# Two-layer adaptive FFN with adapters: the low parts of the token blocks are formed by VectorE instead of GpSimd

## What is computed

```
x = x + ffn0(cond0(x))
    cond0: per item one of 8 weight matrices 512x512 (chosen by itok_B_3_7)
    ffn0:  x @ kernel + bias + per-group low-rank part + shared low-rank part
x = x + ffn1(cond1(x))
    cond1: gate = x @ Wg.T + 0.5*lora ; up = x @ Wu.T + 0.5*lora
           act = silu(gate) * up      ; down = act @ Wd.T + 0.5*lora
           (width 1376; per item one of 16 adapters of rank 16, itok_B_2_6)
    ffn1:  h @ W.T + b + a low-rank part whose rank (8, 16, 32, 64) a router picks per token
```

## Time and profile before

| what | value |
|---|---|
| median of 3 runs | 784.7 us (783.61 to 786.11) |
| the profiled execution, its own time | 782.29 us |
| span of the profiled execution | 780.5 us |
| TensorE busy | 754.0 us, 97% of the span |
| GpSimd busy | 394.7 us, 51% |
| ScalarE busy | 277.3 us, 36% |
| VectorE busy | 272.6 us, 35% |
| mean granted TensorE clock | 0.999 |

### The profile page before, as it was taken

The page is one execution under the profiler, slowest core; times in us unless marked ns, Lnnn a source line. Parts: engine busy times, 40 slices in busy tenths (PEclk is TensorE's granted clock), DMA queues, the critical chain, the costliest instruction groups (busy, mean ns, idle before and its releaser), DMA issues.

```text
span 780.5 us, 11119 instructions
## 1 busy us (share of the span) xinstructions
PE 754.0 (97%) x3902; PEld 625.1 (80%) x3902; DVE 272.6 (35%) x459; ACT 277.3 (36%) x431; POOL 394.7 (51%) x334
## 2 busy tenths in 40 slices
PE   3789999999999999999999999999999999999998
PEld 2567886888888878888888778888888788888885
DVE  4595554421111555211112663111115452111134
ACT  3441262443332424533332435333323334333222
POOL 2177548486674304776664035866642147766500
PEclk9999999999999999999999999999999999999999
DMA  6955455244432331434434041434332324433201
GB/s 261 413 188 190 149 189 217 54 129 122 121 106 85 119 135 40 121 121 121 121 83 165 11 164 60 137 105 121 121 110 78 134 63 128 119 98 120 75 1 55
DMA packets 30873, 96.59 MB, mean 124 GB/s; under 512 B 4832, under 2 KB 4960, under 8 KB 28800
## 3 DMA queue, kind: packets, MB, share of 16 engines
q1 hardware_dynamic: 20544, 61.12, 23.8%
q0 software_dynamic: 10304, 35.14, 14.0%
HBM read 86.28 MB, written 9.96 MB: 123 GB/s over the span
## 4 chain that ended last, share of the span: by engine, by line
PE 90%; DMA 3%; DVE 2%; POOL 2%; issue 1%; ACT 1%; SPq 0%; ACTq 0%; DVEq 0%
PE psD L994 11%; PE psD L995 10%; PE psD L996 10%; PE psG L994 7%; PE psG L996 7%; PE psG L995 7%; PE psU L994 7%; PE psU L996 7%; PE psU L995 7%; PE psD L1055 2%; PE psD L1056 2%; PE psD L1057 2%; DMA xs<-in_x,idx_g 2%; DMA gu_raw<-in_gu 1%; PE psT L996 1%; PE psT L995 1%
## 5 line engine op out<-in xcount | busy, mean ns | idle before, releaser
L440 POOL TENSOR_TENSOR gu_lo<-gu_raw,gu_hi 128x1024 fp32r<-128x1024 f32 x44 | 105.7, 2403 | 180.9 <-ACT gu_hi L566 180.6
L480 POOL DMA_INDIRECT ab<-in_ab,idx_row x88 | 85.9, 976 | 47.7 <-POOL idx_row L474 34.3
L906 DVE TENSOR_TENSOR act_f<-psU,silu 128x512 f32<-128x512 f32 x44 | 30.4, 691 | 222.6 <-PE psU L996 216.5
L680 ACT ACTIVATE silu<-psG 128x512 f32<-128x512 f32 x44 | 26.3, 597 | 181.3 <-PE psG L996 181.1
L440 POOL TENSOR_TENSOR dn_lo<-dn_raw,dn_hi 128x512 fp32r<-128x512 f32 x44 | 56.8, 1291 | 39.3 <-ACT dn_hi L566 39.3
L994 PE MATMUL psG<-x_hi,gu_hi 128*128 128x512 f32 x176 | 72.9, 414 | 0.0
L996 PE MATMUL psG<-x_hi,gu_lo 128*128 128x512 f32 x176 | 69.2, 393 | 0.0
L994 PE MATMUL psD<-act_hi,dn_hi 128*128 128x512 f32 x176 | 69.0, 392 | 0.0
L995 PE MATMUL psD<-act_lo,dn_hi 128*128 128x512 f32 x176 | 69.0, 392 | 0.0
L994 PE MATMUL psU<-x_hi,gu_hi 128*128 128x512 f32 x176 | 68.9, 391 | 0.0
L995 PE MATMUL psG<-x_lo,gu_hi 128*128 128x512 f32 x176 | 68.7, 390 | 0.0
(11 more groups left out here) (264 smaller groups left out, 1837.3 us busy)
## 6 DMA issues: line engine op xcount, KB each, us to landing
gu_raw<-in_gu SPq DMA_DIRECT2D x44, 512.0 KB, 3.5
dn_raw<-in_dn SPq DMA_DIRECT2D x44, 256.0 KB, 2.6
cond_w_raw<-in_cond_w SPq DMA_DIRECT2D x8, 1024.0 KB, 13.1
tok<-h_scratch SPq DMA_DIRECT2D x4, 1024.0 KB, 6.0
x_t<-in_x_t SPq DMA_DIRECT2D x4, 1024.0 KB, 5.4
out_t<-out_b SPq DMA_DIRECT2D x16, 256.0 KB, 3.5
ab<-in_ab,idx_row POOLq DMA_INDIRECT x88, 3.1
lora_a<-in_lora_a SPq DMA_DIRECT2D x1, 1024.0 KB, 5.7
```

Source lines behind the costliest of these rows:

```text
L440: pool.tensor_tensor(dst, x, hi, ALU.subtract).then_inc(s, 1)
L480: pool.indirect_dma_start(ab[:, par, g, :], None, a["ab"], bass.IndirectOffsetOnAxis(idx_row[:, par, g:g + 1], 0)).then_inc(S[f"ab_in{par} ...
L680: act.activation(silu[:], psG[:], ACT.Silu).then_inc(S["silu_s"], 1)
L906: dve.tensor_tensor(act_f[:], psU[:], silu[:], ALU.mult).then_inc(S["act_f_s"], 1)
```

## The change

In the four token blocks VectorE now forms `gu_lo`, `bu_lo`, `dn_lo` and `bd_lo`. GpSimd keeps the indirect DMAs, `ae_lo`, and `wf_lo` and `ra_lo` in its prologue. VectorE gets the wait for `wf_lo_s` ahead of its first block. On VectorE `low_gu(0, ...)` stands between the last `x1_lo` and `ranks(0)`, `bd_lo` behind `ranks(1)`, and in each step `low_gu` of the next chunk stands ahead of `ad_lo`, and `dn_lo` behind it. The steps that VectorE runs outside its loop change from 0 and 1 to 1 and 2, plus the rest that the loop of four leaves. A local name is changed as well (`last` to `copied`), since `last(fc)` is now called there.

```diff
@@ gpsimd
             def body(t, more):
-                def low_gu(par, n):
-                    pool.wait_ge(S["gu_hi_s"], n + 1)
-                    low(gu_lo[:, par, :], gu_raw[:], gu_hi[:, par, :], S["gu_lo_s"])
-                    pool.wait_ge(S["bu_hi_s"], n + 1)
-                    low(bu_lo[:, par], ab[:, par, :, P:STAB], bu_hi[:, par], S["bu_lo_s"])
-
-                low_gu(0, NF * t)
-                pool.wait_ge(S["bd_hi_s"], t + 1)
-                low(bd_lo[:], fix[:, :, 2 * D:FIX], bd_hi[:], S["bd_lo_s"])
-
                 def step(fc, j, par):
                     n = NF * t + fc
-                    if not last(fc):
-                        low_gu(1 - par, n + 1)
-                    pool.wait_ge(S["dn_hi_s"], n + 1)
-                    low(dn_lo[:, par, :], dn_raw[:], dn_hi[:, par, :], S["dn_lo_s"])
                     if not last(fc) and not last(fc, 1):
@@ vector
             for c in range(C):
                 low_h0(0, c)
+            dve.wait_ge(S["wf_lo_s"], 1)
 
             def body(t, more):
...
+                def low_gu(par, n):
+                    dve.wait_ge(S["gu_hi_s"], n + 1)
+                    low(gu_lo[:, par, :], gu_raw[:], gu_hi[:, par, :], S["gu_lo_s"])
+                    dve.wait_ge(S["bu_hi_s"], n + 1)
+                    low(bu_lo[:, par], ab[:, par, :, P:STAB], bu_hi[:, par], S["bu_lo_s"])
...
+                low_gu(0, NF * t)
                 ranks(0)
                 low_at(3)
                 dve.wait_ge(S["tg_lo_s"], 2 * t + 1)
                 ranks(1)
+                dve.wait_ge(S["bd_hi_s"], t + 1)
+                low(bd_lo[:], fix[:, :, 2 * D:FIX], bd_hi[:], S["bd_lo_s"])
 
                 def step(fc, j, par):
                     n = NF * t + fc
+                    if not last(fc):
+                        low_gu(1 - par, n + 1)
                     dve.wait_ge(S["ad_hi_s"], n + 1)
                     low(ad_lo[:, par, :], psX[:, 0:NGT * P], ad_hi[:, par, :], S["ad_lo_s"])
+                    dve.wait_ge(S["dn_hi_s"], n + 1)
+                    low(dn_lo[:, par, :], dn_raw[:], dn_hi[:, par, :], S["dn_lo_s"])
                     dve.wait_ge(S["silu_s"], n + 1)
...
-                chunks(dve, step, 0, 1)
+                chunks(dve, step, 1, 2)
```

More of the change, by code:

```diff
@@ L958, in body @@
                 for k, hi in enumerate(RANKS):
-                    last = dve.tensor_copy(mexp[:, :, lo:hi],
-                                           soft[:, 10, :, k:k + 1].broadcast_to([P, SUB, hi - lo]))
+                    copied = dve.tensor_copy(mexp[:, :, lo:hi],
+                                             soft[:, 10, :, k:k + 1].broadcast_to([P, SUB, hi - lo]))
                     lo = hi
-                    last.then_inc(S["mexp_s"], 1)
+                    copied.then_inc(S["mexp_s"], 1)
                 dve.wait_ge(S["mask_ps"], SUB * (t + 1))
```

## The result

| | median | runs | ratio to before (95%) |
|---|---|---|---|
| before | 785.07 us | 783.61 to 786.11, 4 runs | |
| after | 795.91 us | 794.61 to 797.28, 4 runs | 1.0138 [1.0121, 1.0155] |

The change costs 10.8 us. The forecast was 794.3 with 9.6 us of loss and a range of 789.5 to 798. The profiled execution after has a span of 792.7 us and its own time is 794.61; before it was 780.5 and 782.29.

A forecast was written before the change was run, and what follows sets the result against it. TensorE was taken to bound the kernel. Terms of 3.5 + 0.7 + 5.4 = 9.6 us of loss, added to the 784.7 us median, gave 794.3 us, with a range of 789.5 to 798.

The forecast's parts named there:

- The bound: Blocks 1 to 3: TensorE busy throughout, nothing to win; its 3.0 us of block 0 waits is about all the gain.
- Place 1: VectorE's new wait for wf_lo ahead of block 0: TensorE stalls 6.9 us, less 3.4 of old waits, +3.5 us once.
- The start of `wf_lo`: GpSimd prologue: wf_lo may start 0.5 us earlier, as the gather ahead no longer meets r_lo; end taken as 127.15.
- Place 2: gu_lo(0) and bu_lo(0) ahead of ranks(0) on VectorE: TensorE's ranks(1) weight load late, 0.2 a block, +0.7 us for four.
- Place 3: ad_lo(0) behind bd_lo, gu_lo(1) and bu_lo(1) on VectorE: TensorE's turn_down waits 1.36 us a block, +5.4 us for four.
- Steps 2 to 10: Later chunk steps of each block: gu_lo(n+1) is ready a step early, cost 0.
- the load of `gu_raw`: SP's next gu_raw load, sent after gu_lo(0), goes out later but is covered with 2.0 us to spare, cost 0.
- GpSimd's freed time: Some 230 us of work removed from GpSimd, which no TensorE step waits for in steady state; worth nothing in itself.
- the gathers: GpSimd's gathers: VectorE subtractions delay them at most 1.3 us a time, hidden because they are issued earlier.

The follow-up runs named there:

- e3: Changed kernel with VectorE's wf_lo wait directly ahead of gu_lo(0), ad_lo ahead of gu_lo and bu_lo in every step, and bd_lo behind the chunks; 783.18 us.
- e8: Kernel before with bd_lo alone moved from GpSimd to VectorE, behind the chunks, no new wait for wf_lo; 782.93 us.
- e4: Kernel before with VectorE's wait for wf_lo ahead of block 0 as the only edit; 791.33 us.
- e2: Changed kernel with ad_lo ahead of gu_lo and bu_lo in every VectorE step and bd_lo behind the chunks, wf_lo wait left in place; 791.19 us.
- e1: Changed kernel with VectorE's wait for wf_lo moved from ahead of the block body to directly ahead of gu_lo(0); 789.8 us.
- e5: Changed kernel with bd_lo alone moved on VectorE from behind ranks(1) to behind the chunks; 791.4 us.
- e6: Changed kernel with dn_lo ahead of ad_lo in every step, one more instruction ahead of ad_lo(0); 798.25 us.
- e7: Changed kernel with GpSimd forming wf_lo between the gathers of the first and second chunk instead of behind both; 793.29 us.

## Why the prediction was right

**The bound.** TensorE's 100% in blocks 1 to 3 said that nothing could be won there. e3 and e8 bear it out: the best order tried of the same change gains 0.26%, and e3's 1.8 and e8's 2.4 us stay under the 3.0 us that the prediction gave as about all there is.

**Place 1** was forecast at +3.5. By the parts it was 6.7 us of stall (forecast 6.9), less 3.4 of old waits absorbed (as forecast), plus 2.4 us of matmuls at half the clock (6.46 - 4.04), which the sum didn't have: 5.7. By the whole of block 0 it is 6.0 (7.1 longer, less 1.1 at `ad_lo`). e4 says 6.4 for the wait alone; its trace has one later fall of the clock, and the slow stretch in block 0 was longer there (6.9 us from the first column to the second, where the kernel after has 6.46). Against e3, which has the order right, the wait costs e2 more, 8.0 by the medians (791.19 - 783.18) and 7.4 by the blocks, since e3 is 1.3 us under the kernel before in that block (164.1 against 165.5): with `bd_lo` gone from GpSimd block 0 waits less, and the stall hides that. The term that failed is the price of the stall: "a stall of 6.9 us" was priced as 6.9, and here each stall of TensorE cost its length and a stretch of slow matmuls behind it. That the fall of the clock comes with the stall is shown by e4, which adds the stall and gets the fall, and by e1 and e3, which take the stall away and lose it.

**The start of `wf_lo`.** The gather ahead of it took 0.95 us instead of 1.46, and `wf_lo` began 0.97 us after that gather's start, as forecast from the earlier trace rows. Counted from the first transposes of block 0 `wf_lo` ended 0.5 us earlier than before (12.53 against 13.06). The rule of the Trainium skill (SBUF — State Buffer, "Who interferes with whom") that a `tensor_tensor` leaves descriptor generation alone, which the page gives as inferred, doesn't fit here. In the kernel after a gather that began inside VectorE's `bd_lo` took 1.44 us (from two timelines):

```profile
158.46 1.44 POOL L480 DMA_INDIRECT ab<-in_ab,idx_row  x1 [0.30 <-issue]
...
157.86 1.22 DVE L700 TENSOR_TENSOR bd_lo<-fix,bd_hi 128x1024 fp32r<-128x1024 f32 x1
```

It isn't one row any more. Of the 88 `ab` gathers of the kernel after, 30 began while a VectorE subtraction with both inputs in SBUF was running that had 0.15 us or more to go. All 30 are longer (1.01 to 1.51 us), each by the rest of that subtraction less about 0.1; the other 58 took 0.95 to 0.99. In the kernel before there are two such gathers: the one of the earlier trace rows, and one that began only 0.02 us into a subtraction and isn't longer. In e4, where the wait moves `r_lo` away from the gathers, none is longer. Gathers that had begun before the subtraction aren't longer either. So the prediction's reading of that row holds. Why the page's inference fails isn't shown: a gather also reads its indices (`idx_row`) from SBUF, which may be what is held up. The page's other rule, that a VectorE instruction with two SBUF inputs and a GpSimd instruction that reads SBUF exclude each other, is what e8 shows (2.11 to 0.69 us).

**Place 2** was forecast at 0.7 in all and costs under 0.2. The last `at_lo` ended 5.08 us behind the last `x_lo`'s start (317.79 + 0.68 - 313.39), as computed (5.11). TensorE's `ranks(1)` began 5.21 us behind it, just as in the earlier trace rows and the profile before; the weight load came late by 0.15, and the matmul didn't, so the early start of the weight load was slack that I had counted as need.

**Place 3** was forecast at 1.36 a block and is 1.1, 4.4 in all where 5.4 was said. Mechanism and order are as told (`bd_lo`, `gu_lo(1)`, `bu_lo(1)`, then `ad_lo(0)`); the spacing behind a 1024-element subtraction is 1.14 us, not 1.20, which for the two of them is about half of the 0.27 a block that the forecast was too high; the rest lies between the end of `ad_lo` and TensorE's restart. e2, e5 and e6 show the mechanism.

**Costed at nothing, rightly.** Steps 2 to 10 (e3's block of 164.5 us), the load of `gu_raw`, which took part of its 2.0 us of slack (in block 0 `gu_hi(1)` and `bu_hi(1)` ended at 155.3, 1.3 us ahead of `tg_hi(1)`), GpSimd's freed time, the gathers.

**Sum.** 3.5 + 0.7 + 5.4 = 9.6 against 10.8. Two terms were 1.0 and 0.5 too large, one was 2.4 too small. That the total came within 1.2 us is in part luck: with places 2 and 3 at what they turned out to cost, the same working gives about 8.1, and the stretch at half clock is the 2.4 that it lacks.

## What to carry to other kernels

When work moves between engines that are not the bound, the sum of busy times says nothing. Take each wait of the bounding engine, measure how early it is met today, and count what newly stands in that queue ahead of the instruction that meets it: here 103 us of work cost nothing, and one instruction a block in the wrong place (`bd_lo`, e5) 4.4 us. A wait belongs right ahead of the instruction that needs it, since everything written behind it on that engine waits with it: moving this one down by a few lines brought 6 us (e1). And a stall of TensorE of several us is dearer than its length, by what its clock takes to come back: 2.4 to 3.1 us on stalls of 3.6 to 6.7 us here.

## What the runs showed of the hardware

- A pause of TensorE of 3.6 us (e7) already brought the granted clock from 1.00 to 0.50 before work resumed, and the matmuls then ran at half speed for about 5 us (0.63 us each instead of 0.39), much as after the pause of 6.7 us. In e4, e5 and e6 the clock fell about 3 us into the pause (in e2 and the kernel after about 5) and stayed down for over 6 us after work resumed; the first output column took 6.9 to 7.1 us there, the next one 4.0.
- The granted clock also fell where no such stall stands ahead of it: at the border between blocks 2 and 3 in e1 and e4, and in the conditional stage of e3 (0.83 over 70 to 80; the longest pause ahead of it is 0.8 us). It cost e1 about 1.6 us, and isn't tied to the change.
- Two subtractions whose inputs all lie in SBUF, one on VectorE and one on GpSimd, exclude each other: 2.11 us against 0.69 for the same instruction. With one input in PSUM VectorE's runs through (`ad_lo`, 0.42 us).
- A gather (indirect DMA issued by GpSimd) that starts inside a VectorE subtraction with both inputs in SBUF takes longer by about the rest of it: 1.01 to 1.51 us in 30 cases of the kernel after, against 0.95 to 0.99 otherwise.
- A 1024-element `tensor_tensor` is 1.22 us on VectorE and 2.40 on GpSimd; on VectorE the next instruction starts 1.14 us after its start.
